# A graph layer's slot table holds each edge's node beside its row, and a pair's two one-hots become one comparison

## The reference

```python
row, col = src, dst                                   # 25000 edges, 50000 nodes, D = 256
h = concatenate([x[row], x[col]], axis=-1)
msgs = silu(h @ W1.T + b1) @ W2.T + b2
agg = segment_sum(msgs, row, num_segments=n_nodes)    # sum of the messages of each node
cnt = segment_sum(ones, row, num_segments=n_nodes)
agg = agg / (cnt + 1e-08)
gi = agg @ w_ih.T + b_ih
gh = x @ w_hh.T + b_hh                                # then the gates r, z, n of a GRU
x_new = (1.0 - z) * n + z * x
y = gamma * (x_new - mean) / sqrt(var + 1e-05) + beta
out = layernorm(x + y)
```

## Time and profile before

| | |
|---|---|
| runs before | 2405.72 us, median of 3 (2403.91 to 2411.65) |
| profiled execution | 2403.31 us, its span 2401.6 us |
| busy over the span | PE 2185.4 us (91%), DVE 1999.3 (83%), ACT 1539.8 (64%), POOL 1742.8 (73%) |
| mean granted TensorE clock | 0.976 of full speed |
| DMA | 528.22 MB, mean 220 GB/s |

### The profile page before, as it was taken

The page is one execution under the profiler, slowest core; times in us unless marked ns, Lnnn a source line. Parts: engine busy times, 40 slices in busy tenths (PEclk is TensorE's granted clock), DMA queues, the critical chain, the costliest instruction groups (busy, mean ns, idle before and its releaser), DMA issues.

```text
span 2401.6 us, 48711 instructions
## 1 busy us (share of the span) xinstructions
PE 2185.4 (91%) x10620; PEld 1667.8 (69%) x10620; DVE 1999.3 (83%) x6515; ACT 1539.8 (64%) x3158; POOL 1742.8 (73%) x1824
## 2 busy tenths in 40 slices
PE   6898998899898989889999999999999999999995
PEld 4777777777777777666666666676676667666763
DVE  6776776667676666669999999999999999999998
ACT  3444444444444444558888888888888888887876
POOL 5656666666666656468888888888888888888885
PEclk9999999999999999989999999999999999999998
DMA  5666666666566656657767677666666676766763
GB/s 159 219 222 211 217 231 211 219 211 227 207 230 217 215 202 215 225 198 227 237 232 227 227 235 238 228 236 222 228 231 228 230 235 226 239 232 224 234 215 131
DMA packets 206647, 528.22 MB, mean 220 GB/s; under 512 B 58696, under 2 KB 67680, under 8 KB 206608
## 3 DMA queue, kind: packets, MB, share of 16 engines
q1 hardware_dynamic: 124168, 320.62, 38.3%
q0 software_dynamic: 81600, 206.79, 26.9%
q10 hardware_dynamic: 840, 0.40, 0.1%
HBM read 475.46 MB, written 207.08 MB: 284 GB/s over the span
## 4 chain that ended last, share of the span: by engine, by line
PE 26%; DVE 24%; issue 19%; DMA 12%; POOL 8%; another core or an unknown queue 7%; ACT 2%; DVEq 1%; POOLq 0%; SPq 0%; ACTq 0%
PE banks L1086 23%; DMA mg<-messages,rows_now 11%; DVE tg L1028 4%; POOL mg L391 4%; DVE st L1064 3%; DVE uu L1039 3%; PE banks L1102 3%; DVE diff L1011 3%; DVE oh L990 2%; DVE zd L1016 2%; POOL xb L515 1%; DVE msg L779 1%; DMA xts<-in_xt 1%; POOL rs L531 1%
## 5 line engine op out<-in xcount | busy, mean ns | idle before, releaser
L1086 PE MATMUL banks<-whh,xts 128*128 128x512 f32 (+1 forms) x1568 | 561.5, 486 | 0.0
L391 POOL DMA_INDIRECT mg<-messages,rows_now x392 | 449.9, 1148 | 94.4 <-issue 86.0
L1086 PE MATMUL banks<-mg,oh 128*128 128x512 f32 (+1 forms) x1568 | 322.4, 348 | 78.3 <-DVE npre L1005 50.3
L587 ACT ACTIVATE msg<-banks 128x512 fp32r<-128x512 f32 (+1 forms) x392 | 187.0, 493 | 321.6 <-PE banks L1086 174.9
L1086 PEld LDWEIGHTS banks<-mg,oh 128*128 128x128 f32 x1568 | 253.3, 189 | 182.9 <-issue 128.1
L1086 PEld LDWEIGHTS banks<-whh,xts 128*128 128x128 f32 x1568 | 269.4, 189 | 151.8 <-issue 141.4
L391 POOL DMA_INDIRECT xsrc<-in_x,src_now x196 | 192.1, 980 | 243.4 <-PE banks L1102 113.6
L1086 PE MATMUL banks<-wsh,silh 128*128 128x512 f32 (+1 forms) x784 | 278.7, 356 | 80.8 <-DVE msg L779 77.2
L658 ACT ACTIVATE banks<-banks,rcount 128x768 f32<-128x768 f32 x392 | 326.5, 871 | 27.9 <-PE banks L1086 16.6
L779 DVE TENSOR_TENSOR msg<-banks,msg 128x512 fp32r<-128x512 f32 (+1 forms) x392 | 203.9, 552 | 163.5 <-ACT msg L587 129.1
L1086 PE MATMUL banks<-wsl,silh 128*128 128x512 f32 (+1 forms) x784 | 273.8, 349 | 0.0
(11 more groups left out here) (139 smaller groups left out, 5495.4 us busy)
## 6 DMA issues: line engine op xcount, KB each, us to landing
messages<-msg SPq DMA_DIRECT2D x196, 772.0 KB
xts<-in_xt SPq DMA_DIRECT2D x196, 256.0 KB
xs<-in_x SPq DMA_DIRECT2D x196, 256.0 KB
out_y<-yy SPq DMA_DIRECT2D x196, 256.0 KB
near<-tile_blocks SPq DMA_DIRECT2D x49, 128.0 KB
mg<-messages,rows_now POOLq DMA_INDIRECT x392
xsrc<-in_x,src_now POOLq DMA_INDIRECT x196
xdst<-in_x,dst_now POOLq DMA_INDIRECT x196
```

Source lines behind the costliest of these rows:

```text
L391: nc.gpsimd.indirect_dma_start(out=dst_tile, out_offset=None, in_=rows, in_offset=bass.IndirectOffsetOnAxis(ap=table, axis=0), bounds_chec ...
L587: nc.scalar.activation(msg[:, u % EU, n0:n1], p_g[:, part, 0:n1 - n0], ACT.Copy).then_inc(e_gh[part], 1)
L1086: return nc.tensor.matmul(out_, lhsT, rhs, start=start, stop=stop, skip_group_check=skip)
```

## The change

1. The table's entry becomes row x 256 + node within the block + 1. `place_row[:, 1, :]` is computed accordingly, a little later in the setup, and an empty slot is EMPTY x 256, whose node is 0.
2. At the handover DVE splits the table: `slot_low` by a bitwise and, `slot_row` by a shift in place (now `tab_ready`), `slot_node` by a copy to f32. POOL waits for `tab_ready` where it waited for `st_got`.
3. `one_hot` becomes one TENSOR_TENSOR of 126 x 256 elements that compares `iota1` with `slot_node`. It no longer waits for the gathers. `segment_sum` on PE waits for them instead, with one semaphore for both halves. `copy_rows` waits for earlier gathers to land where it waited for earlier one-hots.
4. In the edge stage `got_src` and `got_dst` become one semaphore, and so do `e_sil` and `e_sh`.

```diff
-            nc.vector.tensor_copy(place_row[:, 1, :], cst[:, C_ROW:C_ROW + TILES]).then_inc(st_empty, 1)
...
             dve.wait_ge(idx_ready, N_IDX)
+            nc.vector.scalar_tensor_tensor(out=place_row[:, 1, :], in0=cst[:, C_ROW:C_ROW + TILES], scalar=float(1 << NODE_BITS),
+                                           in1=locf[:, :], op0=ALU.mult, op1=ALU.add).then_inc(st_empty, 1)
...
-            pool.wait_ge(st_got, 16)
+            pool.wait_ge(tab_ready, 1)
...
-                        need(pool, S["n_oh"], q - QU + 2)
+                        if not isinstance(q, int) or q >= QU:
+                            pool.wait_ge(got_m[u], 32 * nth(q, u))
+                            pool.wait_ge(got_m[u + 1], 32 * nth(q, u))
...
-                dve.wait_ge(e_sh[m], k + 1)
-                dve.wait_ge(e_sil[m], k + 1)
+                dve.wait_ge(e_sh[m], k * 2 + 2)
...
-                    nc.vector.tensor_scalar(slot_used[:, :], slot_row[:, :], float(EDGES_PAD), None, ALU.is_lt)\
+                    nc.vector.tensor_scalar(slot_low[:, :], slot_row[:, :], (1 << NODE_BITS) - 1, None, ALU.bitwise_and)\
+                        .then_inc(tab_step, 1)
+                    nc.vector.tensor_scalar(slot_row[:, :], slot_row[:, :], NODE_BITS, None, ALU.arith_shift_right)\
                         .then_inc(tab_ready, 1)
+                    dve.wait_ge(tab_step, 1)
+                    nc.vector.tensor_copy(slot_node[:, :], slot_low[:, :]).then_inc(tab_step, 1)
...
-                for h in range(2):
-                    need(dve, S[f"n_sg{h}"], q - QU + 1)
-                    dve.wait_ge(got_m[2 * u + h], 16 * (nth(q, u) + 1))
-                    last = nc.vector.tensor_scalar(oh[0:SLOTS, u, h, :], iota1[0:SLOTS, :],
-                                                   mg[0:SLOTS, u, h, LOC:LOC + 1].bitcast(f32),
-                                                   slot_used[0:SLOTS, bass.ds(q * 2 + h, 1)], ALU.is_equal, ALU.mult)
-                last.then_inc(S["n_oh"], 1)
+                need(dve, S["n_sg1"], q - QU + 1)
+                of = slot_node[0:SLOTS, bass.ds(q * 2, 2)].rearrange("p (h a) -> p h a", a=1)
+                nc.vector.tensor_tensor(oh[0:SLOTS, u, :, :], iota1[0:SLOTS, :].rearrange("p (a l) -> p a l", a=1)
+                                        .to_broadcast([SLOTS, 2, P]), of.to_broadcast([SLOTS, 2, P]), ALU.is_equal)\
+                    .then_inc(S["n_oh"], 1)
...
-                pe.wait_ge(got_src[u % XE], 16 * nth_)
-                pe.wait_ge(got_dst[u % XE], 16 * nth_)
+                pe.wait_ge(got_xe[u % XE], 32 * nth_)
...
                 pe.wait_ge(S["n_oh"], q + 1)
+                pe.wait_ge(got_m[u], 32 * (nth(q, u) + 1))
```

More of the change, by code:

```diff
@@ L33 @@
 EMPTY = float(1 << 20)
+NODE_BITS = 8
 T_LOW = 8
@@ L100, in gnn_layer @@
         slot_used = sb("slot_used", [P, BLOCKS])
+        slot_node, slot_low = sb("slot_node", [P, BLOCKS]), sb("slot_low", [P, BLOCKS], i32)
         rcount = sb("rcount", [P, BLOCKS])
@@ L182, in gnn_layer @@
         idx_now = sem("idx_now")
-        got_src, got_dst, e_stored = sems("got_src", XE), sems("got_dst", XE), sems("e_stored", EU)
+        got_xe, e_stored = sems("got_xe", XE), sems("e_stored", EU)
         e_xt, e_hi, e_lo = sem("e_xt"), sem("e_hi"), sem("e_lo")
-        e_hid, e_sil, e_sh, e_sl = sems("e_hid", KC), sems("e_sil", KC), sems("e_sh", KC), sems("e_sl", KC)
+        e_hid, e_sh, e_sl = sems("e_hid", KC), sems("e_sh", KC), sems("e_sl", KC)
         e_g, e_gh, e_gl, e_loc = sems("e_g", 2), sems("e_gh", 2), sems("e_gl", 2), sem("e_loc")
@@ L191, in gnn_layer @@
         pool_passed, dve_passed, sp_passed = sem("pool_passed"), sem("dve_passed"), sem("sp_passed")
-        tab_ready, rc_step, rc_ready = sem("tab_ready"), sem("rc_step"), sem("rc_ready")
+        tab_ready, tab_step, rc_step, rc_ready = sem("tab_ready"), sem("tab_step"), sem("rc_step"), sem("rc_ready")
         node_const, mg_zero = sem("node_const"), sem("mg_zero")
@@ L201, in gnn_layer @@
         got_c = sems("got_c", QU)
-        got_x, got_xt, got_m, n_stored = sems("got_x", QU), sems("got_xt", QU), sems("got_m", 2 * QU), sems("n_stored", QU)
+        got_x, got_xt, got_m, n_stored = sems("got_x", QU), sems("got_xt", QU), sems("got_m", QU), sems("n_stored", QU)
         names = ("n_oh n_sg0 n_sg1 n_sc0 n_sc1 n_g0 n_g1 n_mm n_rz0 n_rz1 n_rhn n_npre n_tanh n_diff n_xb n_zd n_xn"
@@ L399, in _ @@
             last_place = pool.to_reg(SLOTS * BLOCKS - 1)
-            nc.gpsimd.memset(slot_row[:, :], int(EMPTY)).then_inc(st_empty, 1)
+            nc.gpsimd.memset(slot_row[:, :], int(EMPTY) << NODE_BITS).then_inc(st_empty, 1)
             pool.wait_ge(ld_e, 32)
@@ L420, in indices @@
                 for u in range(XE):
-                    need(pool, got_dst[u], 16 * (n + (-1)))
+                    need(pool, got_xe[u], 32 * (n + (-1)))
                 nc.gpsimd.tensor_copy(src_now[:, side, :], srci[:, bass.ds(n * XE, XE)]).then_inc(idx_now, 1)
@@ L428, in gather_edges @@
                     need_apart(pool, pool_passed, e_xt, n * XE + (u - XE + 1))
-                    gather(xsrc[:, u, :], src_now[:, side, u:u + 1], x, got_src[u])
-                    gather(xdst[:, u, :], dst_now[:, side, u:u + 1], x, got_dst[u])
+                    gather(xsrc[:, u, :], src_now[:, side, u:u + 1], x, got_xe[u])
+                    gather(xdst[:, u, :], dst_now[:, side, u:u + 1], x, got_xe[u])
                     if u == XE - 1:
@@ L498, in gather_rows @@
                             nc.gpsimd.dma_start(to, sums[h][bass.ds(q * P, P), :])\
-                                .then_inc(got_m[2 * u + h], 16)
+                                .then_inc(got_m[u], 16)
                         else:
-                            gather(to, rows_now[:, 2 * u + h:2 * u + h + 1], messages, got_m[2 * u + h], last_row)
+                            gather(to, rows_now[:, 2 * u + h:2 * u + h + 1], messages, got_m[u], last_row)
                 def x_lo(q, u):
@@ L576, in edge_silu @@
                 need(act, e_sl[m], k)
-                nc.scalar.activation(sil[:, m, :], p_hid[:, m, :], ACT.Silu, bias=b1s[:, m:m + 1]).then_inc(e_sil[m], 1)
+                nc.scalar.activation(sil[:, m, :], p_hid[:, m, :], ACT.Silu, bias=b1s[:, m:m + 1]).then_inc(e_sh[m], 1)
                 need(act, e_g[1], k * QUAD - QUAD)
@@ L916, in _ @@
             edge_slots(dve, edge_slot, first=QUAD, also=tail)
+            dve.wait_ge(tab_step, 2)
             dve.wait_ge(tab_ready, 1)
@@ L981, in _ @@
                                                 ALU.subtract).then_inc(v_add, 1)
-                nc.vector.memset(slot_used[:, :], 1.0).then_inc(tab_ready, 1)
+                nc.vector.tensor_scalar(slot_node[:, :], cst[:, C_BLOCK:C_BLOCK + BLOCKS], 0.0, cst[:, C_PART:C_PART + 1],
+                                        ALU.mult, ALU.add).then_inc(tab_ready, 1)
                 dve.wait_ge(tab_ready, 2)
             def one_hot(q, u):
-                for h in range(2):
-                    need(dve, S[f"n_sg{h}"], q - QU + 1)
-                    dve.wait_ge(got_m[2 * u + h], 16 * (nth(q, u) + 1))
-                    last = nc.vector.tensor_scalar(oh[0:SLOTS, u, h, :], iota1[0:SLOTS, :],
-                                                   mg[0:SLOTS, u, h, LOC:LOC + 1].bitcast(f32),
-                                                   slot_used[0:SLOTS, bass.ds(q * 2 + h, 1)], ALU.is_equal, ALU.mult)
-                last.then_inc(S["n_oh"], 1)
+                need(dve, S["n_sg1"], q - QU + 1)
[3 more added lines that the diff above has]
+                    .then_inc(S["n_oh"], 1)
             def gated_h(q, u):
@@ L1120, in edge_hidden @@
                     pe.wait_ge(e_lo, k * QUAD + QUAD)
-                    need(pe, e_sh[m], k)
+                    need(pe, e_sh[m], k * 2)
                 o = p_hid[:, m, :]
```

## The result

The kernel after takes 2336.0 us (median of 4, 2333.36 to 2339.78) against 2404.81 before (median of 4): a ratio of 0.9714, 95% interval 0.9685 to 0.9743, 69 us less. The forecast was 2343 us, with a range of 2328 to 2374. The profiled execution has a span of 2331.7 us, 69.9 less than the one of before.

The account below looks back on a forecast made before the run. DVE was taken to bound the node stage. Moved wait -30.5, comparison -32.8, handover +0.2 and setup +0.2 sum to -62.9 us: 2403.3 profiled becomes 2340.4, and with 2.4 for the median 2343 us, range 2328 to 2374.

Parts of the forecast that it names:

- The bound: Node stage: DVE sets the pace; its turn falls to 6.53 us, above PE's floor of 6.32 and POOL's 6.16.
- The comparison: Node stage, DVE: one instruction of 0.34 us replaces two one-hots of 0.51, saving 0.17 a turn, 32.8 us in all.
- the Trainium skill's mode rule: DVE: fp32 tensor_scalar runs two elements a cycle, tensor_tensor one; the prediction estimated 12 us saved from it instead of 33.
- The moved wait: Node stage: the wait for gathered rows moves from DVE to PE, which asks 3.35 us later; all 30.5 us go.
- Handover and setup: Table split before the node stage: POOL's gathers start 0.7 us later, first pair 0.5 less, net +0.2; setup another +0.2.
- Edge stage: Merged semaphores in the edge stage remove queue work but gain 0, with a bound of -5 us.
- The comparison not cheaper: Rival, DVE: broadcast reads or the slower mode make the comparison cost 0.51 (2376 us) or 0.45 (2364 us); 13%.
- PE at 6.66: Rival, node stage: PE needs its present 6.66 us a turn, so most of DVE's gain is lost, 2368 us; 8%.
- Late gathers on PE: Rival, node stage: gathers land too late for PE instead, so all 30.5 us come back, 2373 us; 5%.
- The comparison waiting for rs: Rival, node stage: DVE's comparison waits for the end of POOL's rs, 215 us lost, 2558 us; 5%.
- POOL slipping behind: Rival, node stage: POOL's copy is delayed, xb comes later and holds nmr on DVE, 29 us back, 2372 us; 9%.
- My floor of 6.16 for POOL: Node stage: POOL's shortest mean turn, about 6.853 us less 0.69 of waiting for tg.

Follow-up runs that it names:

- two_two_scalars: Kernel after with the comparison made by two TENSOR_SCALARs with two pointer scalars each, as before, without the wait for gathers on DVE; ratio to before 0.9835.
- after_again: The kernel after, unchanged, run once more on chip 7; ratio to before 0.9716, 2206.23 us.
- edge_semaphores: Kernel after with the merged semaphores of the edge stage taken apart again; ratio to before 0.9713.
- load_x_mean_on_act: Kernel after with SP's load of transposed x one lag earlier and minus the mean computed on ACT instead of DVE; ratio to before 0.9625, 2186.58 us.
- short_beta_on_pool: load_x_mean_on_act with POOL's addition of beta cut from 512 to 8 columns from the fifth pair on (output wrong); ratio to before 0.9512.

## Why the prediction was right

**The bound.** DVE sets the pace before: right, and the forecast's mechanism holds. With the wait gone and DVE 0.17 shorter the turn is 6.532, forecast 6.53. PE's 95% of busy time was no bound; its floor, read from the early turns as 6.32, is 6.31. Two of the signs were off in size: PE's wait for npre nearly vanished (2.8 us) where it was to become more even, and POOL waits 52.9 / 195 = 0.27 us a turn for tg, not 0.5. PE's 0.2 us of slack a turn is not seen in its busy time, whose ends are modelled.

**The comparison.** Forecast 0.34 start to start, measured 0.33 to 0.34. The saving from two_two_scalars to after_again is 31.9 us of the stretch, forecast 32.8; in the timed ratios it is 1.19%, 27 us of 2271. What I made of the Trainium skill's mode rule was wrong, though, not the rule: I gave the new instruction the fixed cost of the old one, 0.19, which holds two pointers that the new one does not have. With 0.07 the rule gives the row.

**The moved wait.** Forecast 30.5 us, all of it gone. From before to two_two_scalars the stretch is 33.5 us shorter, and the timed ratio has 1.65% or 38 us; at the new comparison it is 1.88% or 43 us. So by the timed runs the wait was priced some 7 us too low and the comparison some 6 too high, each no more than the intervals (0.25%, 6 us) leave open; that the two miss in opposite directions is luck. PE has no measured wait for rows in the steady part. The margin is as forecast: the latest recorded landing comes 1.5 us before segment_sum starts in after and in after_again, forecast 1.4. In edge_semaphores one pair has only 0.4 us, so the margin is not wide.

**Handover and setup.** Forecast +0.2 with POOL 0.7 later. tab_ready comes at about 1012.2 and POOL is not later: its pause, 4.6 us before and 4.5 after, covers it. The other half, PE's first start at the landing, came as said: -0.5 in all. Both are differences between single executions.

**Edge stage.** Forecast 0, bound -5; measured -6.3 in one execution each, and 0 in timed runs with the merges undone. So the forecast of 0 holds, and the 6.3 us are chance as far as these runs tell.

**The rivals.** The comparison not cheaper: excluded by two_two_scalars. PE at 6.66: excluded, 6.31. Late gathers on PE: none. The comparison waiting for rs: line 1002 has a maximum of 421 ns over 196 instructions, nearly all of which start while rs or the copy runs on POOL. POOL slipping behind: not at 6.53, where nmr has a mean of 237 ns after 227 before, but at 6.42 to 6.44.

My floor of 6.16 for POOL was too low. It took the idle time off the turn as if POOL's work were fixed, and as if POOL held the turn only by being busy. Neither is so. The medians of POOL's own work change: the small copy's is 0.50 us in before and after and 0.22 in load_x_mean_on_act, that of issuing a gather 1.05, 1.07 and 1.35. And DVE's nmr stands until xb has ended, in before already: the prediction saw this in one turn, as an example, and left it out of "DVE runs without a gap". How the missing 0.26 is shared out among these was not tested. Had DVE's turn been foreseen at 6.40, the forecast would have failed at this point.

The profiled span was 2331.7 against the 2338.7 that the sum gives (2401.6 - 62.9); nearly all of the difference is the edge stage's 6.3. On chip 7 the kernel after is 2271.0 - 2206.2 = 64.8 us faster, against 62.9 forecast.

## What to carry to other kernels

Ask of every wait for a DMA on the engine that sets the pace whether the data is needed there at all. Here one column of each gathered row was, and carrying it in the index table let the wait go to a step that stands 3.35 us later. Price such a wait at the pace that the kernel will have: it may grow as the engine gets faster (30.5 us at the old pace, 43 to 48 at the new one here). For small DVE instructions count start to start, here 0.07 us and 0.06 for each pointer scalar, before counting elements. After a gain ask who waits no longer: POOL's lost waits named the next bound, and a version with one more step off DVE and one load moved up gave another 0.9%. And look for instructions that last longer than their elements ask for: a tiny one that ends together with another engine's large one is a wait that no list of waits shows.

## What the runs showed of the hardware that was not expected

The edge stage of one and the same kernel ends near 878 us on chip 7 and between 1005 and 1029 us elsewhere, while the node stage agrees within 0.5% (1271.0 to 1276.9 us). From 20 to 870 us PE is busy for 842 us at a granted clock of 1.00 in after_again, and for 765 at 0.97 in after, with 245 and 213 GB/s. What makes the difference was not looked into.

nmr on DVE has 2 elements a lane. It starts while POOL's addition xb, which reads two operands from SBUF, is running. In the traces before and after it ends 15 to 24 ns behind xb's end in 175 of 177 steady turns. Its durations (min/median/max ns) in load_x_mean_on_act and, without most of xb, in short_beta_on_pool:
```profile
L1070 DVE TENSOR_TENSOR nmr<-nm,rs x196: 130/310/1219, 949.5 to 2182.0; 128x2 f32<-128x2 f32 x196
L1071 DVE TENSOR_TENSOR nmr<-nm,rs x196: 131/152/161, 1088.2 to 2294.2; 128x2 f32<-128x2 f32 x196
```
With the long addition gone the waiting is gone, so xb is what holds nmr.

tg has two SBUF operands of 256 elements, and POOL's rs never holds it up: it lasts 468 to 483 ns beside it in before (1043 to 2380). Only at the end of that trace one of its two instructions starts just behind an xb, and there it is held too, 1.49 us in place of 0.47 (the row has both together):
```profile
2387.33 1.88 DVE L1028 SCALAR_TENSOR_TENSOR tg<-xn,ag,gammab 128x256 f32<-128x256 f32 x2
2387.66 1.27 POOL L515 TENSOR_TENSOR xb<-xs,betab 128x512 f32<-128x512 f32 x1
...
2389.14 0.15 DVE L1059 TENSOR_TENSOR nmr<-nm,rs 128x2 f32<-128x2 f32 x1
```
The same DVE instruction is thus held by one POOL instruction of 1.27 us (xb) and not by another of 1.0 to 1.35 (rs). What an instruction on POOL holds is not told by its length in the profile.
